# Gating and output taken into the last feed-forward chunk in place, and that chunk's layer norm issued within the chunk ahead of it

## The chip, the cores and the metric

The kernel runs on one core of a Trainium2 chip. The metric is the device time of one execution in microseconds (us), lower is better. A core has five engines that run their own instruction streams and meet at semaphores: TensorE (PE in the rows; its weight loads are PEld), VectorE (DVE), ScalarE (ACT), GpSimd (POOL) and SyncE (SP), which here only issues DMA transfers. Matrix products land in PSUM, everything else lies in SBUF.

## The reference, cut to what matters

Four sequences of 1024 tokens with 256 features go through a layer norm, then two branches: a global attention over all tokens, and a stack of two local layers. The branch outputs meet in a gate.

```python
# x: (4, 1024, 256)
xn = layernorm(x)
s = attn(xn, w_qkv, w_out)           # global attention, 16 heads
t = xn
for l in range(2):                   # the local layers
    t = t + local_attention(shift_token(t)) @ wo[l]
    h = shift_token(t)
    h = (h - mean(h)) / sqrt(var(h) + 1e-05) * lg + lb
    a, g = split(h @ w1 + b1)        # 2 * 682 columns
    t = t + (a * gelu(g)) @ w2 + b2
out = x + s * silu(t)
```

The names are shortened here; the last line is the part that the change moves.

## The kernel before, in words

The 4096 tokens are 8 chunks of 512 columns (`CHUNKS`), each four windows of 128. The stream `t` is held transposed, features on partitions, in `xnt`, a tile of 2 halves (`KD`) by 8 chunks by 513 columns. Four stages follow each other: `prepare_tokens`, `global_attention`, `local_layers` and `combine`. Between two stages stands a barrier of all engines, and the tiles of a stage are given back at its end.

**local_layers.** Its loop runs over rounds g. A round has four window steps w = 0 to 3. Round g projects the queries, keys and values of chunk g (of 16, 8 for each of two layers), works its attention, and does the second half, the feed-forward part, of chunk g - 2. So the last two rounds, g = 16 (`LAST`) and g = 17, project nothing: round 16 still has the ends of the last attention windows and the feed-forward part of the layer's chunk 6, and round 17 has only the feed-forward part of chunk 7. `PLAN` lists the rounds, and in each engine's `body` hand-written conditions say what that engine issues in a step, and in what order. There is no scheduler: the order of the code is the order of the engine.

The feed-forward part of a chunk, by its functions: `output_product` (8 products of `wo` with the attention output into PSUM banks `ffn0`, `ffn1`), `add_attention` (VectorE, sum with `xnt` into `mid`), `mean` (a product with `mean_w`), `centre` (VectorE), `square_deviations` (ScalarE), `variance` (a product), `inverse_deviation` (ScalarE, Ln then Exp with scale -0.5), `scale` and `shift` (VectorE, on `centred`, then a split into `f_high` and `f_low`), five `hidden_tile`s f = 0 to 4, each with 6 products into `ffn0` for the gate half and 6 into `ffn1` for the other, `tails` (6 products), and two `down`s m = 0, 1 with 6 products each. ScalarE turns each gate half by Gelu (`gate_tile`), VectorE multiplies (`hidden_tile`), and `add_ffn` adds the down product to `mid` and writes it to `xnt`. The fp32 products (`wo`, `mean_w`, `w2`) are two instructions each in the rows, those of the split operands one. In round 17 each of these steps waits for the one before it.

**The two PSUM banks** go round: `ffn_ready` and `ffn_taken` count the fills and the reads of each bank, with 9 uses of bank 0 and 8 of bank 1 in a round (`USES`). A fill waits until its bank's last use was taken.

**combine** starts after the barrier. SyncE loads the attention output `s` of chunks 6 and 7 and `x` of chunks 6 and 7 (the other six of each were loaded during the last rounds into the places of weights and tables no longer needed, `early_s` and `early_x`). ScalarE makes silu of each half of a chunk, VectorE multiplies half 0 with `s` and GpSimd half 1 (`gated`), TensorE turns the 8 squares of 128 by 128 back into PSUM, VectorE adds `x` into `result`, and SyncE stores 512 KB of output. `silu`, `gated`, `result` and the PSUM tiles have two buffers each, so chunk n waits for chunk n - 2, in `result` for its store.

## Time and profile before

| | us |
|---|---|
| median of 3 runs | 2339.86 |
| lowest, highest | 2337.14, 2340.36 |
| the profiled execution | 2328.96 |
| its span, first to last instruction | 2327.2 |
| its mean granted TensorE clock | 0.971 of full speed |

| engine | busy us | share of the span |
|---|---|---|
| TensorE | 2195.7 | 94% |
| VectorE | 1621.7 | 70% |
| ScalarE | 1380.5 | 59% |
| GpSimd | 610.5 | 26% |

The span counts from the first instruction to the last; the profiled execution's own time has 1.8 us around it. All the times inside a kernel below are us from the start of the span. A row gives start, duration, engine, line and operation, output and inputs, and in brackets the idle time of the engine before it and what ended that. Instructions of an engine overlap a little: two VectorE operations of 0.69 take 1.29 together. "x8" joins eight instructions of a kind.

### The profile page before, as it was taken

The numbers are of one execution on the slowest core, as the hardware profiler recorded it, in microseconds if no ns is written. First come the engines' busy times: TensorE is split into PE (matmuls) and PEld (weight loads), VectorE is DVE, ScalarE is ACT, GpSimd is POOL, SyncE is SP. The second block draws the span as 40 slices with busy tenths as digits, with TensorE's granted clock in tenths as the row PEclk, the third lists the DMA queues.
The fourth block names the chain that finished last, engine by engine and source line by source line (L and its number), as shares of the span: only waits on it lengthen the run. The fifth ranks groups of instructions, "written<-read, shape, count | busy, mean of one in ns | idle before, by whom it ended". The sixth has DMA issues, their size and how long they took to land. (4 is left out here: it accounts for less than half of the span.)

```text
span 2327.2 us, 43427 instructions
## 1 busy us (share of the span) xinstructions
PE 2195.7 (94%) x14592; PEld 1288.5 (55%) x14592; DVE 1621.7 (70%) x3789; ACT 1380.5 (59%) x2551; POOL 610.5 (26%) x490
## 2 busy tenths in 40 slices
PE   7869999999999979899999999899999999999976
PEld 4533333333333336566666666666666676676644
DVE  5768999999999936655666666556666656666534
ACT  2215888888888845555655555555555565565533
POOL 3521200000000024333332333332432333333201
PEclk9977999999999989999999999999999999999988
DMA  4585122211112022200000000000100000000303
GB/s 135 183 252 159 52 64 65 65 56 60 57 53 63 29 80 103 88 10 1 1 0 0 0 0 0 27 1 10 36 1 1 1 0 0 0 0 0 108 1 109
DMA packets 76984, 108.96 MB, mean 47 GB/s; under 512 B 14204, under 2 KB 49360, under 8 KB 76752
## 3 DMA queue, kind: packets, MB, share of 16 engines
q1 hardware_dynamic: 76864, 107.30, 14.4%
q8 instruction: 82, 1.34, 0.3%
q14 instruction: 38, 0.31, 0.0%
HBM read 68.74 MB, written 43.95 MB: 48 GB/s over the span
## 5 line engine op out<-in xcount | busy, mean ns | idle before, releaser
L669 DVE TENSOR_REDUCE maxima<-ps_m 128x1 f32<-128x512 f32 x1024 | 629.1, 683 | 20.7 <-PE ps_m L549 16.6
L737 ACT ACTIVATE probs<-ps_st 128x1024 f32<-128x1024 f32 x512 | 521.1, 1025 | 161.7 <-PE ps_st L576 142.6
L549 PE MATMUL ps_m<-k_st,q_st 48*128 48x512 f32 x1024 | 392.4, 466 | 19.9 <-DMA k_st<-ks 15.6
L1355 ACT ACTIVATE l_probs<-l_probs,l_neg_max 128x256 f32<-128x256 f32 x512 | 254.0, 498 | 194.5 <-DVE l_neg_max L1514 194.5
L576 PE MATMUL ps_st<-q_st,k_st 50*128 50x512 f32 x1024 | 367.5, 444 | 2.0 <-DMA q_st<-max_rows 1.6
L592 PE MATMUL ps_o<-probs,v_st 128*32 128x256 f32 x4096 | 322.1, 392 | 0.1
L1514 DVE CUSTOM_DVE_ANT_1 l_probs<-ring,l_mask 128x256 f32<-128x256 f32 x384 | 140.0, 421 | 198.5 <-PE ring L1123 198.0
L576 PEld LDWEIGHTS ps_st<-q_st,k_st 50*128 50x128 f32 x1024 | 154.5, 186 | 194.0 <-issue 173.8
L1334 ACT COPY p_turned<-ring 128x512 f32<-128x512 f32 x256 | 140.4, 599 | 163.7 <-PE ring L1083 163.6
L1042 POOL TENSOR_SCALAR clipped<-sumsq 128x16 f32<-128x16 f32 x64 | 16.2, 253 | 766.9 <-DVE sumsq L1481 766.9
L549 PEld LDWEIGHTS ps_m<-k_st,q_st 48*128 48x128 f32 x1024 | 166.7, 190 | 53.3 <-DVE maxima L669 31.5
L1044 POOL TENSOR_TENSOR inv_norm<-clipped,halves 128x16 f32<-128x16 f32 x64 | 187.6, 2931 | 5.3
L592 PEld LDWEIGHTS ps_o<-probs,v_st 128*32 128x32 f32 x4096 | 84.1, 108 | 169.5 <-ACT probs L737 110.4
L1573 DVE SCALAR_TENSOR_TENSOR hidden<-ffn,b_l,gate 128x512 f32<-128x512 f32 x96 | 71.9, 749 | 147.2 <-PE ffn L1137 72.3
L1137 PE MATMUL ffn<-hidden,w_l 128*128 128x512 f32 x384 | 172.6, 600 | 0.0
L1526 DVE TENSOR_SCALAR l_probs<-l_probs,l_inv_total 128x256 f32<-128x256 f32 x512 | 166.3, 388 | 4.5
L1046 POOL TENSOR_TENSOR rope_a<-rope_a,rope_b 128x1024 f32<-128x1024 f32 x64 | 157.0, 2453 | 0.0
L1083 PE MATMUL ring<-l_ident,l_probs 128*128 128x128 f32 x1024 | 142.2, 280 | 13.6 <-DVE l_probs L1526 13.6
L1095 PE MATMUL l_ps_o<-p_turned,v_ring 128*64 128x128 f32 x2048 | 149.5, 284 | 5.3 <-ACT p_turned L1334 5.3
L1137 PE MATMUL ffn<-f_high,w_high 128*128 128x512 f32 x352 | 148.1, 421 | 5.7 <-DVE f_low L1564 5.6
L1095 PEld LDWEIGHTS l_ps_o<-p_turned,v_ring 128*64 128x64 f32 x2048 | 110.2, 138 | 66.0 <-issue 53.3
L508 POOL TENSOR_TENSOR max_hl<-row_max,zeros 128x16 fp32r<-128x16 f32 x32 | 7.1, 222 | 531.8 <-DVE row_max L678 531.8
(156 smaller groups left out, 3864.7 us busy)
## 6 DMA issues: line engine op xcount, KB each, us to landing
qs<-split SPq DMA_DIRECT2D x16, 512.0 KB, 3.5
ks<-split SPq DMA_DIRECT2D x16, 512.0 KB, 5.1
q_st<-qs SPq DMA_DIRECT2D x64, 128.0 KB, 2.5
k_st<-ks SPq DMA_DIRECT2D x64, 128.0 KB, 3.1
o<-o_sb SPq DMA_DIRECT2D x32, 256.0 KB, 2.3
hidden<-o SPq DMA_DIRECT2D x17, 256.0 KB, 6.6
x_in<-in_L_attn_x_dram SPq DMA_DIRECT2D x8, 512.0 KB, 5.6
v<-v_sb SPq DMA_DIRECT2D x16, 256.0 KB, 4.7
```

The costliest lines, as they stand in the source:

```text
L549: nc.tensor.matmul(bank(base, use)[:, :], q_st[u][r, qt * P:(qt + 1) * P], k_st[u][r, h * CH:(h + 1) * CH], start=True, stop=True).then_in ...
L576: mm = nc.tensor.matmul(ps_st[j][:, h * CH:(h + 1) * CH], k_st[u][r, kt * P:(kt + 1) * P], q_st[u][r, h * CH:(h + 1) * CH], start=True, st ...
L592: mm = nc.tensor.matmul(ps_o[r:r + 32, q], v_st[:, kt, 2 * u + j, :], probs[:, kt % 4, j, h * CH + q.start:h * CH + q.stop], start=(kt == ...
L669: nc.vector.tensor_reduce(maxima[:, par, side(e), tile + e // 4, e % 2:e % 2 + 1], bank(base, k + e)[:, :], AX_X, ALU.max).then_inc(m_used, 1)
L737: nc.scalar.activation(probs[:, kt % 4, j, :], ps_st[j][:, :], ACT.Exp, scale=float(G_DIM) ** -0.5).then_inc(exp_done, 1)
L1044: nc.gpsimd.tensor_tensor(inv_norm[:, :], clipped[:, :], halves[:, :], ALU.pow).then_inc(inv_done, 1)
L1046: nc.gpsimd.tensor_tensor(rope_a[:, :, :], rope_a[:, :, :], rope_b[:, :, :], ALU.add).then_inc(added, 1)
L1083: mm = nc.tensor.transpose(ring[(PT + p) % 2][:, (2 * j + s) * P:(2 * j + s + 1) * P], probs[:, 2 * p + j, s * P:(s + 1) * P], wt.ident[:, :])
L1095: mm = nc.tensor.matmul(ps_o[j * HDIM:(j + 1) * HDIM, p * P:(p + 1) * P], v_ring[:, slot, head * HDIM:(head + 1) * HDIM], p_turned[:, p % ...
L1137: mm = nc.tensor.matmul(ffn[bank][:, :], a, b, start=(n == 0), stop=(n == len(operands) - 1))
L1355: nc.scalar.activation(probs[:, head, :], probs[:, head, :], ACT.Exp, bias=neg_max[:, head:head + 1], scale=-1.0, accum_out=total[:, head: ...
L1526: ins = nc.vector.tensor_scalar(probs[:, head, :], probs[:, head, :], inv_total[:, head:head + 1], None, ALU.mult)
```

## The change

Three things are done, all in `local_layers`, and the stage `combine` is gone, with the barrier ahead of it.

- **The layer norm of chunk 7** is issued within round 16. `late(g)` is true for round 17, and then the steps from `output_product` to `shift` use other places: PSUM `ps_q`, `ps_k`, `ps_v` and `l_ps_o` in the place of `ffn0` and `ffn1`, `l_mid` (in the attention's `probs`), `l_centred` (`qk_n`), squares in `k_ring`, and `h_high`, `h_low` for `f_high`, `f_low`. TensorE has `late_output` after hidden tile 3 of round 16, `late_mean` after its tails, and `late_variance` between its two downs.
- **The gate** is written in place: silu and the product with `s` both overwrite `xnt`. ScalarE makes silu of chunks 0 to 3 at the end of round 16, and of chunks 4 to 7 at the end of round 17. GpSimd multiplies both halves of chunks 0 to 3 and half 1 of chunks 4 to 6, VectorE half 0 of chunks 4 to 6 and both of chunk 7. `s` of chunks 6 and 7 goes to `o_ring`, `x` of them to `v_ring`.
- **The turning back, the sum and the store** of chunks 0 to 5 stand between the products of round 17: `turn_back(n)` on TensorE, `add_x(n)` on VectorE, in place into the room of `x`, from where SyncE stores. Two of the four PSUM tiles are the attention's `ring0` and `ring1`, two are `ps_q` and `ps_k`.

Two loads of ScalarE's function table (in round 16 at w = 2, and in round 17) are left out, and three others (silu, Gelu, silu) stand where the silus are.

```diff
+        def nth(g, bank, use):
+            return (g - 2) * USES[bank] + use - (2 if late(g) else 0)
+        back = ((ring[0], ring[1]), (ps_q, ps_k))
...
                 run(pool, body)
+                for n in range(4):
+                    for k in range(KD):
+                        gate_back(n, k)
+                for n in range(4, CHUNKS - 1):
+                    gate_back(n, 1)
...
                         if forward and w == 3:
                             hidden_tile(g, lf, 4)
+                        if late(g) and w == 3:
+                            turn_back(2)
...
                         if forward and w == 2:
                             hidden_tile(g, lf, 2)
+                        if late(g) and w == 2:
+                            turn_back(0)
                         if forward and w == 3:
                             tails(g, lf)
+                        if late(g) and w == 3:
+                            turn_back(3)
...
                         if forward and w == 2:
                             hidden_tile(g, lf, 3)
+                        if last_but_one and w == 2:
+                            late_output()
+                        if late(g) and w == 2:
+                            turn_back(1)
+                        if last_but_one and w == 3:
+                            late_mean()
                         if forward and w == 3:
                             down(g, lf, 0)
+                        if late(g) and w == 3:
+                            turn_back(4)
+                            turn_back(5)
+                        if last_but_one and w == 3:
+                            late_variance()
...
                         if forward and w == 3:
                             down(g, lf, 1)
+                        if late(g) and w == 3:
+                            turn_back(6)
+                            turn_back(7)
...
+                for n in range(CHUNKS):
+                    sp.wait_ge(summed, 2 * n + 2)
+                    dst = out[n // 2, n % 2 * CH:(n % 2 + 1) * CH, :].rearrange("(t p) n -> p t n", p=P)
+                    sp.dma_start(dst, x_room(n)).then_inc(out_stored, 16)
...
-                        if w >= 2 and forward:
+                        if w >= 2 and forward and (mid_ or isinstance(g, int) and g == LAST and w == 3):
                             nc.scalar.preload_act_table_set(EXP_LN)
...
+                        if isinstance(g, int) and g == LAST and w == 3:
+                            square_deviations(g + 1)
+                            inverse_deviation(g + 1)
+                            nc.scalar.preload_act_table_set(SILU)
+                            for n in range(4):
+                                silu(g, n)
+                            nc.scalar.preload_act_table_set(GELU)
+                        if late(g) and w == 3:
+                            nc.scalar.preload_act_table_set(SILU)
+                            for n in range(4, CHUNKS):
+                                silu(g, n)
...
+                def gate_back(n, k):
+                    attention_in(dve, n)
+                    dve.wait_ge(silu_done[k], n + 1)
+                    nc.vector.tensor_tensor(xnt[:, k, n, 1:], attention(n, k), xnt[:, k, n, 1:], ALU.mult).then_inc(gated_done[k], 1)
+
+                def add_x(n):
...
+                    for m in range(2):
+                        dve.wait_ge(turned_back, 2 * n + m + 1)
+                        room = x_room(n)[:, 2 * m:2 * m + 2, :].rearrange("p t n -> p (t n)")
+                        nc.vector.tensor_tensor(room, back[n % 2][m][:, :], room, ALU.add).then_inc(summed, 1)
...
+                        if late(g) and w == 3:
+                            add_x(0)
                         if forward and w == 3:
                             hidden_tile(g, lf, 4)
...
+                        if late(g) and w == 3:
+                            add_x(1)
                         if forward and w == 3:
                             hidden_tile(g, lf, FT)
+                        if late(g) and w == 3:
+                            add_x(2)
+                            add_x(3)
+                            for k in range(4, CHUNKS - 1):
+                                gate_back(k, 0)
...
                         if forward and w == 3:
                             add_ffn(g, lf, n, 0)
+                        if late(g) and w == 3:
+                            add_x(4)
+                            gate_back(CHUNKS - 1, 0)
+                            add_x(5)
+                        if last_but_one and w == 3:
+                            scale(g + 1, lf)
+                            shift(g + 1, lf)
+                        if forward and w == 3:
                             add_ffn(g, lf, n, 1)
-                            carry(g, n)
+                            if late(g):
+                                add_x(6)
+                                gate_back(CHUNKS - 1, 1)
+                                add_x(7)
+                            else:
+                                carry(g, n)
```

TensorE at the end of chunk 6 and the start of chunk 7, before. `ffn<-o_ring,wo_l` is the output product, the two with `mean_w` are mean and variance, `ffn<-hidden,w_l` are the downs, and `ffn<-f_high,w_high` with `normed` opens chunk 7's hidden tile 0.

```order
L1137 MATMUL ffn<-hidden,w_l 128x512 [waits ffn_taken0,ffn_taken1]
...
L1137 MATMUL ffn<-o_ring,wo_l 128x512 [waits ffn_taken0,o_out]
...
L1137 MATMUL ffn<-mid,mean_w 128x512 [waits ffn_taken0,ffn_taken1]
...
L1137 MATMUL ffn<-hidden,mean_w 128x512 [waits ffn_taken1,sq_dev]
...
L1137 MATMUL ffn<-f_high,w_high 128x512 [waits ffn_taken0,normed]
```

The same place in the changed kernel:

```order
L1221 MATMUL ps_q<-o_ring,wo_l 128x512 [waits l_roped,o_out]
...
L1221 MATMUL ps_v<-l_probs,mean_w 128x512 [waits late_mid,v_out]
...
L1199 MATMUL ffn<-hidden,w_l 128x512 [waits ffn_taken1]
...
L1221 MATMUL l_ps_o<-k_ring,mean_w 128x512 [waits sq_dev]
...
L1199 MATMUL ffn<-hidden,w_l 128x512 [waits ffn_taken0,ffn_taken1]
...
L1199 MATMUL ffn<-h_high,w_high 128x512 [waits ffn_taken0,normed]
```

The three products of the norm now stand ahead of the second down, and nothing stands between that down and chunk 7's first tile but the wait for `normed` and bank 0.

VectorE at the same place in the changed kernel, from the centring of chunk 7 on. The last `xnt<-ffn` row is `add_ffn(16, 1)`, which frees bank 0.

```order
L1728 SCALAR_TENSOR_TENSOR qk_n<-ps_v,l_probs 128x512 [waits late_ready]
...
L1763 SCALAR_TENSOR_TENSOR xnt<-ffn,b_l,mid 128x512 [waits ffn_ready1]
L1737 TENSOR_TENSOR qk_n<-qk_n,dev 128x512 [waits sq_dev,dev_done]
...
L1742 TENSOR_SCALAR qk_n<-qk_n,lnp_l 128x512 [waits l_scaled] x2
L1746 CAST h_high<-qk_n 128x512 [waits shifted_done] x2
L1749 TENSOR_TENSOR h_low<-qk_n,h_high 128x512 [waits f_high_done] x2
L1763 SCALAR_TENSOR_TENSOR xnt<-ffn,b_l,mid 128x512 [waits ffn_ready0]
```

The scaling, shifting and splitting of chunk 7 stand between chunk 6's two sums, and chunk 6's second sum stands behind them.

ScalarE in the changed kernel, at the turn from round 16 to 17, from the Ln of chunk 7's variance (`dev<-l_ps_o`) and the Exp behind it to the first Gelu of chunk 7.

```order
L1512 ACTIVATE dev<-l_ps_o,eps_col 128x512 [waits late_ready]
L1518 ACTIVATE dev<-dev 128x512 [waits late_ln]
L1592 ACT_TABLE_LOAD
L1526 ACTIVATE xnt<-xnt 128x512 [waits x_out] x8
L1595 ACT_TABLE_LOAD
L1533 ACTIVATE gate<-ffn,b_l 128x512 [waits ffn_ready0] x5
```

Eight silus and two table loads now stand ahead of the first Gelu. GpSimd's first eight products wait for one of these silus each, and for nothing else that is late.

## Rows read from the trace of the kernel before

**Rows 1.** Busy time in four stretches: stretch, length, engines, TensorE clock, DMA.
```profile
2223.10:2249.20 26.10, 26.10 (x92) 16.77 (x90) 5.26 (x7) 9.85 (x11) 0.00 (x0) 1.00 0.00 0
2249.20:2270.70 21.50, 11.66 (x25) 4.31 (x24) 7.86 (x15) 3.75 (x5) 0.00 (x0) 0.84 0.00 1
2270.70:2298.40 27.70, 27.65 (x90) 17.98 (x90) 5.26 (x7) 7.98 (x9) 0.00 (x0) 0.94 0.00 0
2298.40:2327.20 28.80, 11.77 (x64) 9.55 (x64) 18.07 (x26) 10.31 (x17) 11.19 (x8) 0.73 0.66 219
```

**Rows 2.** Chain that ended last, by line, of 2200 to 2327.
```profile
by line: DMA out_dram<-result 9.8%; DVE result L1756 2.3%; PE ps_t L1776 1.5%; issue 1.1%; ACT L1725 1.0%; POOL gated L1734 1.0%; ACT silu L1725 0.9%; DVEq L1703 0.5%; DVEq L1755 0.1%; DVE gated L1743 0.0%; POOLq L1731 0.0%
```

**Rows 3.** Timeline: TensorE's products of rounds 16 and 17.
```profile
2203.30 1.88 PE L1137 MATMUL ffn<-mid,mean_w 128*128 128x512 f32 x4
...
2223.11 0.50 PE L1137 MATMUL ffn<-f_high,w_high 128*128 128x512 f32 x1
...
2234.44 0.50 PE L1137 MATMUL ffn<-f_high,w_high 128*128 128x512 f32 x1
...
2238.76 10.46 PE L1137 MATMUL ffn<-hidden,w_l 128*128 128x512 f32 x24
...
2250.15 7.10 PE L1137 MATMUL ffn<-o_ring,wo_l 128*128 128x512 f32 x16 [0.94 <-DVE xnt L1578]
```

**Rows 4.** Timeline: chunk 7's norm, from the variance product on.
```profile
2262.60 2.58 PE L1137 MATMUL ffn<-hidden,mean_w 128*128 128x512 f32 x4 [2.56 <-ACT hidden L1368]
...
2265.23 0.69 ACT L1374 ACTIVATE dev<-ffn,eps_col 128x512 f32<-128x512 f32 x1 [2.67 <-PE ffn L1137]
2265.95 0.63 ACT L1376 ACTIVATE dev<-dev 128x512 f32<-128x512 f32 x1
...
2266.61 1.29 DVE L1552 TENSOR_TENSOR hidden<-hidden,dev 128x512 f32<-128x512 f32 x2 [5.24 <-ACT dev L1376]
...
2268.73 0.75 DVE L1561 CAST f_high<-hidden 128x512 fp32r<-128x512 f32 x2
2269.40 1.28 DVE L1564 TENSOR_TENSOR f_low<-hidden,f_high 128x512 fp32r<-128x512 f32 x2
...
2270.74 0.79 PE L1137 MATMUL ffn<-f_high,w_high 128*128 128x512 f32 x1 [5.55 <-DVE f_low L1564]
```

**Rows 5.** Timeline: VectorE and GpSimd at once, in combine, then in prepare_tokens.
```profile
2302.40 1.27 POOL L1734 TENSOR_TENSOR gated<-wqkv_high,silu 128x512 f32<-128x512 f32 x1 [117.37 <-ACT silu L1725]
2302.88 1.34 DVE L1743 TENSOR_TENSOR gated<-wqkv_high,silu 128x512 f32<-128x512 f32 x1 [0.35 <-ACT silu L1725]
2303.63 1.73 POOL L1734 TENSOR_TENSOR gated<-wqkv_high,silu 128x512 f32<-128x512 f32 x1
...
63.82 0.40 DVE L195 TENSOR_SCALAR xn<-x_in,moments,rstd 128x256 f32<-128x256 f32 x1
...
63.94 0.76 POOL L150 COPY xnt<-xs 128x512 f32 x1
64.14 0.70 DVE L195 TENSOR_SCALAR xn<-x_in,moments,rstd 128x256 f32<-128x256 f32 x1
...
64.64 0.68 POOL L150 COPY xnt<-xs 128x512 f32 x1
...
64.76 0.70 DVE L195 TENSOR_SCALAR xn<-x_in,moments,rstd 128x256 f32<-128x256 f32 x1
```

**Rows 6.** Timeline: ScalarE's table load and silus at the start of combine.
```profile
2299.81 1.28 ACT L1725 ACT_TABLE_LOAD   x1 [9.70 <-PEq L1022]
...
2301.11 3.78 ACT L1725 ACTIVATE silu<-xnt 128x512 f32<-128x512 f32 x7
```

**Rows 7.** TensorE alone, columns as in Rows 1: its clock and instructions.
```profile
2270.00:2272.00 2.00, 1.26 (x3) 0.50 0.00 0
2272.00:2274.00 2.00, 2.00 (x6) 0.50 0.00 0
2274.00:2276.00 2.00, 2.00 (x10) 0.98 0.00 0
```

**Rows 8.** Timeline: chunk 7's last sum, a chunk's transposes, the last output sums.
```profile
2298.43 0.75 DVE L1578 SCALAR_TENSOR_TENSOR xnt<-ffn,b_l,mid 128x512 f32<-128x512 f32 x1 [4.40 <-PE ffn L1137]
...
2309.60 1.09 PE L1776 MATMUL ps_t<-l_ident,gated 128*128 128x128 f32 x8 [0.53 <-DVE gated L1743]
...
2320.90 2.56 DVE L1756 TENSOR_TENSOR result<-ps_t,x_late 128x512 f32<-128x512 f32 x4 [2.60 <-issue]
```

More of the change, by code:

```diff
@@ L1186, in body @@
                 def body(g, la, lf, before_hidden=None):
+                    last_but_one = isinstance(g, int) and g == LAST
                     for w in range(WPC):
@@ L1202, in body @@
                             turn_probs(W, 1)
-                        if forward and w == 0:
+                        if forward and w == 0 and not late(g):
                             output_product(g, lf)
@@ L1215, in body @@
                             turn_probs(W, 3)
-                        if forward and w == 0:
+                        if forward and w == 0 and not late(g):
                             mean(g)
@@ L1242, in body @@
                             project_o(W - 1)
-                        if forward and w == 0:
+                        if forward and w == 0 and not late(g):
                             variance(g)
@@ L1420, in body @@
                             take_o(g, w)
-                        if forward and w == 0:
+                        if forward and w == 0 and not late(g):
                             square_deviations(g)
@@ L1598, in body @@
                             before_hidden()
-                        if forward and w == 1:
+                        if forward and w == 1 and not late(g):
                             scale(g, lf)
@@ L1613, in body @@
                             take_next(g, la, lf)
-                        if forward and w == 0:
+                        if forward and w == 0 and not late(g):
                             add_attention(g, n)
```

268 lines of the change are left out of this document (143 added, 125 removed).

## The prediction, made before the changed kernel ran

> **What bounds the kernel now.** The change touches only the last 104 us, so I read from the end backwards. The chain of work that ended last shows what the last stage waits for: output stores, 9.8% of the last 127 us, with short pieces of sum, transpose and gate between them [rows 2]. So `combine` is bound by its own pipeline of two buffers, not by one engine. Then the busy times by stretch [rows 1]: chunk 6's tiles and downs take 26.1 us with TensorE full, 21.5 us follow in which TensorE is busy 11.66 (product, sum, mean, centring, variance and norm of chunk 7, one after the other), then 27.7 us of chunk 7's tiles and downs, again full, and 28.8 us from the last down product to the end, in which no engine is busy more than 18.07. The change fills the second stretch and the fourth. The four give 104.1 us, and I work out each anew.
>
> **First stretch: it takes in the norm's products.** Hidden tiles 0 to 3 run from 2223.11 to 2234.44 and the 24 instructions of the downs take 10.46, so 0.43 each [rows 3]. An instruction with `wo` or `mean_w` costs the same: 16 in 7.10, 4 in 1.88 with its overlap. Output product, mean and variance are 16 + 4 + 4 = 24 instructions, 10.3 us, all on TensorE's path. Do they wait? The output product needs only the attention, done before 2223. The mean product needs two VectorE sums, done about 1 us behind the output product, while hidden tile 4 and the tails fill 4.3 us (2234.44 to 2238.76, [rows 3]). The variance needs centring (1.4) and squares (1.2), and the first down, 5.2 us, covers them. So no wait: 26.1 + 10.3 = 36.4 us, and the second down ends at 2249.2 + 10.3 = 2259.5. If a cover were too short by 1 us, it would cost 1 us.
>
> **Second stretch: the gap before chunk 7.** Behind the variance product come Ln, Exp and eight VectorE instructions: from 2265.23 to 2269.40 + 1.28 = 2270.68, 5.45 us [rows 4]. Behind them VectorE has `add_ffn(16, 1)`, 0.75, which frees bank 0, so 6.2 us. The second down covers 5.2 of this. Undisturbed, TensorE would stand 1.1 us.
>
> But it is not undisturbed. Behind Exp ScalarE loads the silu table (1.28) and makes its first silu (0.63), and GpSimd starts 0.14 later [rows 6, 5]: 2.1 us behind Exp, just as the two casts and the two subtractions of the split are due (they begin 2.15 us behind Exp's end, [rows 4]). Two rows show what follows. A VectorE product of two SBUF tiles, begun at 2302.88 while GpSimd's ran from 2302.40 to 2303.67, took 1.34 and not 0.68, and GpSimd's next took 1.73 and not 1.27: they ran one behind the other. In `prepare_tokens` two GpSimd copies and VectorE's TENSOR_SCALARs alternate: VectorE's pitch becomes 0.62 where 0.32 is normal (63.82 to 64.14) [rows 5]. So when both have instructions queued, they take turns. GpSimd has eight products in a row, since silus come every 0.54 (7 in 3.78, [rows 6]) and a product takes 1.27. Four VectorE instructions each behind one of them: 4 x 1.2 = 4.8 us. The bounds: 0, if none is held, and 8 x 1.27 - 2 = about 8 us, if GpSimd lets none through. I take 4.8, since both rows show turns. `add_ffn` and `add_x` have PSUM on one side and are not held: the sums among GpSimd's products took the usual time (2.56 for four, [rows 8]).
>
> The gap is 1.1 + 4.8 = 5.9 us and chunk 7's tiles start at 2265.4 instead of 2270.7. After the old gap of 5.55 us TensorE stood at the lower of its two levels, 1.2 GHz (clock 0.50), till 2274, with 0.43 for an instruction instead of 0.23 for the first eight: 1.6 us, contained in the 27.7 [rows 7]. A gap of 5.9 brings the same again, so nothing changes there.
>
> For the table load the row shows the silu 1.30 us behind its start [rows 6]. The Trainium skill, "ScalarE: Activation LUTs", section "What ACT_TABLE_LOAD costs", adds a drain of about 1.38 us to it, about 2.66 us in all. Where a load has that drain, GpSimd starts behind the split and the sum is 2316.6; that is the fourth case below.
>
> **Third stretch: chunk 7 with six transposes inside.** `turn_back(0)` to `(5)` stand ahead of the second down's end; one takes 1.05 (8 instructions in 1.09 with their overlap, [rows 8]): 6.3 us, all on TensorE's path. 27.7 + 6.3 = 34.0. Their inputs: GpSimd has gated chunks 0 to 3 by about 2270, the first `turn_back` comes near 2275. For chunks 4 to 6 silu begins behind the last Gelu, about 2288, and VectorE must, in its order, finish `add_x(2)`, `add_x(3)` (1.29 each), three gates (0.55 to 1.8 each), `add_ffn(17, 0)`, `add_x(4)`, the gate of chunk 7's half 0 and `add_x(5)` before `add_ffn(17, 1)`, due at 2299.4. Adding these up gives 2298.5: 0.9 us to spare. Queued behind the new waits for `turned_back` in front of hidden tiles 4 and tail are just these products, for which TensorE's first down waits; the transposes come 1 to 3 us earlier, so I cost it at nothing, and at up to 5.7 us if the list runs late. The silus, Gelu loads and GpSimd's eleven products lie beside TensorE's work. SyncE's queue has stores behind loads that were issued long before.
>
> **Fourth stretch: what stays behind the last product.** `add_ffn(17, 1)` 0.75; `add_x(6)` 1.29, which hides the last silu (0.63); the gate of half 1, 0.68; four transposes and their handover 0.65; `add_x(7)` 1.29; from the last sum to the end 3.74 as before (2320.90 + 2.56 = 2323.46, the end at 2327.2, [rows 8]). That is 8.4, less some overlap 8.2, against 28.8. Gone with it are the barrier, the loads of chunks 6 and 7 (issued in round 16, among idle queues) and the wait of `result` for its stores: stores now have a place each.
>
> **The sum.** 36.4 + 5.9 + 34.0 + 8.2 = 84.5 against 104.1: 19.6 us less. The span goes to 2307.6, the profiled execution from 2328.96 to about 2309.4. The median of the runs lies 10.9 us above the profiled execution; I carry that over: 2339.86 - 19.6 = 2320.3.
>
> **The rivals.**
> 1. *They take turns in the split* (forecast): 2320.3, with 2317 to 2323 for its own terms. For it, both rows of [rows 5].
> 2. *The split is not held*, because VectorE's four instructions pass in one turn or GpSimd begins a little later. The gap is about 1 us, and the clock need not fall: 4.8 + 1.6 less, 2313.9. For it: GpSimd's start is only 0.1 us ahead of the casts. Against: the silus follow each other at 0.54 and GpSimd is behind with them throughout.
> 3. *VectorE's list in chunk 7 becomes the bound*: three gates held by GpSimd's again, in front of sums for which TensorE waits. Up to 5.7 us more, 2326. For it: 0.9 us to spare in a list of 11 us. Against: at the tiles of chunk 7 VectorE is busy 5.26 of 27.7 [rows 1].
> 4. *The table load's drain*, a mechanism by which ScalarE is free again only some 1.4 us behind the row's end of a load. Worked out from rows: GpSimd begins that much later, behind the last instruction of the split, so 4.8 + 1.6 are saved; but the first Gelu comes 2 x 1.4 us later, about 2.7 us late for bank 0. 2313.9 + 2.7 = 2316.6. The row's 0.02 us between load and silu speaks against it. The Trainium skill's section named above would have it so.
> 5. *Slower: the lower clock stays for chunk 7.* If short transposes and stalls keep TensorE at 1.2 GHz from 2265 to the end, 66 tile products take 0.2 more each, 24 of the downs 0.43 and 56 transposes 0.13: 31 us, of which 1.6 is already in. 2349. It decides the sign when the low level lasts for two thirds of the chunk. Against: after the same gap the level came back in 3.3 us [rows 7].
> 6. *It does not do what it says*: tiles of chunk 7 wait as late as before and the output still comes in a row behind them; within 0.2% of before. Against: the order of the instructions.
>
> **How the numbers follow.** Chances: 1: 0.52; 2: 0.22; 3: 0.15; 4: 0.03; 5: 0.03; 6: 0.05. What a measurement of this kernel can tell from no change is about 0.2%, 4.7 us. Cases 1 to 4 are faster by more than that, 0.92; case 6 is the same, 0.05; case 5 slower, 0.03. The range leaves out cases 5 and 6 and reaches from case 2 less 3 us to case 3 plus 3 us: 2311 to 2329, some 0.9 of the chance by the cases, cut to 8 in 10 by what moves between executions (3.2 us in three runs).
>
> **What would show it.** Right: a TensorE gap of 5 to 7 us before chunk 7's first tile, ended by VectorE; the two casts or two subtractions there taking 2 to 4 us instead of 2.0 together; 34 us from there to the last down; about 8 us from there to the end. A gap near 1 us is case 2; VectorE's gates ending a wait of a down or of `turn_back(4)` to `(6)` is case 3; a clock of 0.50 beyond 2270 is case 5. It is wrong altogether if stages before 2223 change in length, since no instruction of them does.

## The result, and the profile after

The changed kernel took 2307.01 us (median of four runs, 2300.86 to 2311.05), the kernel before, beside it, 2338.5 (2330.63 to 2340.36). The ratio of the runs is put at 0.9878, with a 95% interval of 0.9854 to 0.9901: 28.5 us less (the two medians lie 31.5 apart), where the prediction had 19.6 less. The direction was right, the size too small, and the time lies below the range of 2311 to 2329.

The profiled execution of the changed kernel took 2310.06 us, with a span of 2308.3. These are its four stretches, cut as in [rows 1] (columns as there): hidden tiles and downs of chunk 6 with the norm's products, gap, tiles and downs of chunk 7, the rest.

```profile
2231.70:2267.90 36.20, 36.20 (x116) 21.40 (x114) 11.80 (x20) 13.39 (x19) 1.58 (x1) 1.00 0.09 29
2267.90:2269.15 1.25, 0.09 (x1) 0.03 (x1) 1.14 (x3) 1.25 (x3) 1.25 (x1) 1.00 0.00 0
2269.15:2300.40 31.25, 31.25 (x140) 22.03 (x141) 17.35 (x24) 11.22 (x17) 12.57 (x11) 1.00 0.26 88
2300.40:2308.30 7.90, 1.96 (x16) 1.48 (x14) 3.90 (x6) 0.63 (x1) 0.00 (x0) 0.88 0.56 189
```

Together 76.6 us against 104.1: 27.5 less, nearly what the runs show. The prediction had 36.4, 5.9, 34.0 and 8.2, or 84.5. So the missing 7.9 us are 4.65 in the gap, 2.75 in chunk 7, 0.3 at the end and 0.2 at the start.

Yet the two spans differ by 18.9 only (2327.2 and 2308.3). The first tile of chunk 6 starts at 2231.67 in this trace and at 2223.11 in [rows 3], and nothing ahead of it is touched by the change. The difference lies between 200 and 300 us. The first line is from the trace of before, the second from that of after:

```profile
200.00:300.00 100.00, 99.57 (x949) 39.67 (x945) 97.42 (x169) 82.96 (x84) 23.34 (x26) 1.00 0.27 81
200.00:300.00 100.00, 99.74 (x853) 38.37 (x849) 87.92 (x151) 74.03 (x75) 23.31 (x26) 0.88 0.21 65
```

TensorE is full in both, but the granted clock is 0.88 and not 1.00, and 96 fewer of its instructions got done. Cut finer, both traces have a clock of 0.50 (1.2 GHz) from 190 to 195 us and of 1.00 (2.4 GHz) from 230 on. What differs is when it rises: between 195 and 200 us before, between 220 and 225 after.

The forecast's doubtful place is the gap ahead of chunk 7. The timeline of the changed kernel's trace shows it (start, duration, engine, line, operation, tiles; in brackets the idle time ahead and who ended it). The two lines in the middle with x2 are the casts and the subtractions of the split:

```profile
2264.25 1.28 ACT L1592 ACT_TABLE_LOAD   x1
2265.47 0.54 DVE L1742 TENSOR_SCALAR qk_n<-qk_n,lnp_l 128x512 f32<-128x512 f32 x1
2265.54 0.63 ACT L1526 ACTIVATE xnt<-xnt 128x512 f32<-128x512 f32 x1
2265.93 0.54 DVE L1742 TENSOR_SCALAR qk_n<-qk_n,lnp_l 128x512 f32<-128x512 f32 x1
2266.32 2.97 POOL L1112 TENSOR_TENSOR xnt<-wqkv_high,xnt 128x512 f32<-128x512 f32 x1 [72.56 <-ACT xnt L1526]
2266.39 0.76 DVE L1746 CAST h_high<-qk_n 128x512 fp32r<-128x512 f32 x2
2267.06 1.29 DVE L1749 TENSOR_TENSOR h_low<-qk_n,h_high 128x512 fp32r<-128x512 f32 x2
2268.26 0.74 DVE L1763 SCALAR_TENSOR_TENSOR xnt<-ffn,b_l,mid 128x512 f32<-128x512 f32 x1
2269.15 0.47 PE L1199 MATMUL ffn<-h_high,w_high 128*128 128x512 f32 x1 [1.16 <-DVE xnt L1763]
2269.26 1.10 POOL L1112 TENSOR_TENSOR xnt<-wqkv_high,xnt 128x512 f32<-128x512 f32 x1
```

GpSimd came where the prediction had it, 0.07 us ahead of the first cast. But VectorE's four instructions took 2.0 us in all, as without it, and GpSimd's product lasted 2.97 instead of 1.1: it ended 0.94 behind the last subtraction. TensorE stood 1.16 us. That is the second case of the prediction (2313.9), to which it gave 0.22.

Some 25 us later, in round 17, the same two engines did take turns, that is, each instruction of one waited for one of the other. VectorE's gate `L1710`, unhindered 0.68, came while GpSimd's product was on. The last line is `add_ffn(17, 1)`, the sum that must not come late:

```profile
2291.34 1.02 DVE L1710 TENSOR_TENSOR xnt<-wqkv_low,xnt 128x512 f32<-128x512 f32 x1
2291.77 1.54 POOL L1112 TENSOR_TENSOR xnt<-wqkv_low,xnt 128x512 f32<-128x512 f32 x1
2292.28 1.57 DVE L1710 TENSOR_TENSOR xnt<-wqkv_low,xnt 128x512 f32<-128x512 f32 x1
2293.27 1.72 POOL L1112 TENSOR_TENSOR xnt<-o_ring,xnt 128x512 f32<-128x512 f32 x1
2293.78 1.76 DVE L1710 TENSOR_TENSOR xnt<-o_ring,xnt 128x512 f32<-128x512 f32 x1
...
2300.43 0.75 DVE L1763 SCALAR_TENSOR_TENSOR xnt<-ffn,b_l,l_probs 128x512 f32<-128x512 f32 x1 [1.24 <-PE ffn L1199]
```

So two questions go to the chip: is the gain in the changed part alone, and what decides between turns and none?

### The profile page after: what moved, and what is told of

The parts are those of the page before. It is cut to its first block, busy times and chain, and to the rows that moved or that the text cites. A ratio compares the mean times of both kernels' runs of the same rounds, so it can differ in the third digit from the quotient of the medians.

```text
span 2308.3 us, 43409 instructions
## 1 busy us (share of the span) xinstructions
PE 2197.8 (95%) x14592; PEld 1287.6 (56%) x14592; DVE 1620.2 (70%) x3785; ACT 1375.1 (60%) x2547; POOL 614.2 (27%) x493
## 3 DMA queue, kind: packets, MB, share of 16 engines
q8 instruction: 82, 1.34, 0.2%
## 4 chain that ended last, share of the span: by engine, by line
PE 51%; DVE 2%; issue 1%; ACT 1%; DVEq 0%; ACTq 0%
PE ffn L1199 24%; PE l_ps_o L1157 5%; PE ring L1145 5%; PE ring L1185 4%; PE ps_v L1132 3%; PE ps_q L1132 3%; PE ps_k L1132 2%; PE ring L1169 2%; PE ring L1187 1%; DVE l_probs L1675 1%; PE ring L1188 0%; ACT k_ring L1481 0%; DVE l_probs L1687 0%; ACT l_probs L1489 0%; PE ps_k L1221 0%
## 5 line engine op out<-in xcount | busy, mean ns | idle before, releaser
L549 PE MATMUL ps_m<-k_st,q_st 48*128 48x512 f32 x1024 | 398.2, 472 | 19.8 <-DMA k_st<-ks 15.6
L576 PE MATMUL ps_st<-q_st,k_st 50*128 50x512 f32 x1024 | 373.3, 450 | 2.3 <-DMA q_st<-max_rows 1.9
L592 PE MATMUL ps_o<-probs,v_st 128*32 128x256 f32 x4096 | 327.4, 398 | 0.1
L1104 POOL TENSOR_TENSOR qk_n<-rope_a,inv_norm 128x1024 f32<-128x1024 f32 x64 | 123.1, 1924 | 84.4 <-PE ring L1169 74.1
```

Of the source, the lines that this page charges most:

```text
L549: nc.tensor.matmul(bank(base, use)[:, :], q_st[u][r, qt * P:(qt + 1) * P], k_st[u][r, h * CH:(h + 1) * CH], start=True, stop=True).then_in ...
L576: mm = nc.tensor.matmul(ps_st[j][:, h * CH:(h + 1) * CH], k_st[u][r, kt * P:(kt + 1) * P], q_st[u][r, h * CH:(h + 1) * CH], start=True, st ...
L592: mm = nc.tensor.matmul(ps_o[r:r + 32, q], v_st[:, kt, 2 * u + j, :], probs[:, kt % 4, j, h * CH + q.start:h * CH + q.stop], start=(kt == ...
```

## Experiments on where the gain is

**The changed kernel again.**

> The changed kernel once more, beside the others, as their control. If the 27.5 us between the two traces (from chunk 6's first tile to the end, 104.1 before and 76.6 after) are what the change gives, that stretch is 76 to 77.5 us again, whatever the stages before it take in this execution, and the time is 26 to 30 us under the kernel before's. If instead the 8.6 us by which the stages before chunk 6's tiles were longer in the changed kernel's trace are a cost of the change, chunk 6's first tile starts near 2231.7 again and not near 2223.

It took 2303.74 us against 2332.84, ratio 0.9877 (0.9848 to 0.9907). Its first tile of chunk 6 starts at 2225.38, its span is 2302.0: 76.6 us again, with 36.31, 1.16, 31.25 and 7.90. Between 200 and 300 us its clock was 0.98.

In the eight traces of this study that hold the whole computation, the start of chunk 6's tiles goes with this one number: clock 1.00, start 2223.1; 0.98, 2225.0 and 2225.4; 0.95, 2226.7; 0.91, 2229.7; 0.87 to 0.89, 2231.7 to 2233.0. All runs' spans agree: those of the kernel before, less 104.1, put this start at 2221 to 2233, and those of the changed kernel, less 76.6, at 2222 to 2233 (an estimate that takes the last stretches as fixed). The 8.6 us are thus an execution's own, and no cost of the change. What decides when this clock rises in an execution, no run here shows.

**The norm ahead, the output stage as before.** Everything of the gating is taken out of the last chunk, and `combine` put back:

```diff
-                for n in range(4):
-                    for k in range(KD):
-                        gate_back(n, k)
...
-                        if late(g) and w == 3:
-                            add_x(0)
...
+            combine(nc, wt, x, x_early, xnt, s_dram, s_stored, out)
```

> The layer norm of chunk 7 ahead, in its new places, and the output stage as it was before (silu, product, transposes and sums in a stage of their own behind the last chunk). By the additive theory the four stretches are 36.2, 1.3, 26.1 (27.7 less the 1.6 of the lower clock, and no transposes) and 28.8: 92.4 against 104.1, so 11.7 us less than before. A rival: with no silu table load and no products of GpSimd beside VectorE's norm chain the gap is shorter than 1.25 us (below 1.0), if these had cost anything there.

The cut shows only a part: all silus, products with `s`, transposes, sums and stores are out of `local_layers`. It took 2320.55 us, ratio 0.9943 (0.9925 to 0.9962). The stretches:

```profile
2232.35:2268.67 36.32, 36.32 (x116) 21.45 (x114) 11.89 (x20) 11.02 (x14) 0.00 (x0) 1.00 0.00 0
2268.67:2269.82 1.15, 0.00 (x1) 0.03 (x1) 1.04 (x3) 0.00 (x0) 0.00 (x0) 1.00 0.00 0
2269.82:2295.76 25.94, 25.94 (x90) 16.84 (x90) 5.45 (x8) 4.12 (x6) 0.00 (x0) 1.00 0.00 1
2295.76:2323.00 27.24, 12.39 (x65) 10.49 (x64) 18.77 (x26) 10.30 (x17) 11.34 (x8) 0.77 0.69 231
```

They add up to 90.65 us, 13.4 less than before (11.7 were expected). The gap is 1.15 without a product of GpSimd and without a silu: they cost nothing there. Chunk 7 takes 25.94, and 27.7 less the 1.6 of the lower clock is 26.1. With this row the changed kernel's 31.25 gives the price of the six groups of transposes: 5.31, 0.89 each. The output stage took 27.24 and not 28.8. The chains that ended last differ there by one output store: in the kernel before it lasts 4.36 us (from 2317.73), while no store of norm_only's chain lasts over 2.91. Why that one was long stays open.

**Gating in place, the norm where it was.**

```diff
+                        if late(g) and w == 0:
+                            late_output()
+                            late_mean()
+                            late_variance()
...
-                        if last_but_one and w == 2:
-                            late_output()
...
+                            nc.scalar.preload_act_table_set(EXP_LN)
+                            square_deviations(g + 1)
+                            inverse_deviation(g + 1)
```

> Silu, product, transposes and sums within chunk 7, its layer norm where it was before (behind the silus of chunks 0 to 3). By the additive theory: 26.1, 21.5, 27.7 + 6 x 0.87 = 32.9 and 7.9: 88.4 against 104.1, 15.7 us less; with norm_only's 11.7 this is the whole 27.5. Against that: GpSimd's eight products now run beside the norm's VectorE instructions from its first sums on, not beside the last ones. If whoever streams first holds the other in turns, the norm's VectorE instructions of two SBUF tiles (centring's and split's) take 1.3 to 1.8 instead of 0.7, and the second stretch is 24 to 27 us.

It took 2315.76 us, ratio 0.9918 (0.9892 to 0.9944). The first stretch is 26.02, the last 7.83, and the two between them:

```profile
2259.05:2278.85 19.80, 10.81 (x25) 4.05 (x23) 8.49 (x15) 3.75 (x5) 1.64 (x2) 0.96 0.01 1
2278.85:2312.47 33.62, 33.62 (x140) 23.88 (x141) 17.17 (x23) 9.27 (x14) 4.28 (x3) 0.92 0.24 81
```

That is 87.3 us in all, 16.8 less (15.7 were expected). The silus ran at 2250.79 and GpSimd's products were over at 2260.7, ahead of the norm's instructions (from 2262.5 on), so nothing was held, and the dearer second stretch that its expectation allowed for did not come. This run tells nothing of turns. Its first product of GpSimd, after 56.61 us of idleness, took 1.09: the 2.97 in the changed kernel is no slow start. The second stretch is 1.7 shorter than before. Of this 0.94 is the wait ahead of the output product [rows 3], which is gone since the norm's products have banks of their own. Another 0.6 is the variance product: 1.98 us at a clock of 1.00, against 2.58 before [rows 4], where the clock fell to 0.62 in its course. The gap ahead of chunk 7 is 5.55, as before, and chunk 7 pays the lower clock again: 33.62.

The two halves give 13.4 and 16.8, the whole 27.5. The 2.7 too many are the 1.6 of norm_only's output stage and the 1.7 of gate_only's second stretch, less 0.6 in chunk 7. The gain is where the prediction put it.

## Experiments on who waits for whom

**VectorE and GpSimd alone.** VectorE's streams of eight against GpSimd's five products.

> Nothing of the computation is left but a copy of x to the output; beside it VectorE and GpSimd run streams against each other: eight VectorE instructions on 128x512 float32 tiles of one kind (products back to back; products each waiting for its predecessor; copies to fp32r; two copies and two subtractions in turn; TENSOR_SCALARs; products with one operand in PSUM) against five GpSimd products of SBUF tiles, once with VectorE ahead by two instructions and once with GpSimd ahead by one. Theory A (the kind decides: VectorE's back-to-back instructions let none of GpSimd's through): VectorE's mean is 0.65 to 0.70 in the phases with both orders and GpSimd's first product lasts as long as VectorE's stream. Theory B (who streams first decides): with VectorE ahead its instructions take their usual time and GpSimd's wait; with GpSimd ahead VectorE's take 1.3 to 1.8. Theory C (turns always, as forecast): both orders show VectorE at 1.3 to 1.8 and GpSimd at 1.7. With an operand in PSUM all expect VectorE undisturbed.

They took turns in every phase but those with an operand in PSUM, whoever came first. These rows are from the products that each wait for the one before and from the casts, GpSimd coming second in both:

```profile
24.62 0.69 DVE L59 TENSOR_TENSOR v_plain<-va,vb 128x512 f32<-128x512 f32 x1
25.34 0.69 DVE L59 TENSOR_TENSOR v_plain<-va,vb 128x512 f32<-128x512 f32 x1
25.48 1.67 POOL L88 TENSOR_TENSOR g_res<-ga,gb 128x512 f32<-128x512 f32 x1 [4.58 <-DVE v_plain L59]
26.07 1.63 DVE L59 TENSOR_TENSOR v_plain<-va,vb 128x512 f32<-128x512 f32 x1
...
46.10 0.42 DVE L65 CAST v_rounded<-va 128x512 fp32r<-128x512 f32 x1
46.36 1.28 POOL L88 TENSOR_TENSOR g_res<-ga,gb 128x512 f32<-128x512 f32 x1 [4.42 <-DVE v_rounded L65]
46.44 1.48 DVE L65 CAST v_rounded<-va 128x512 fp32r<-128x512 f32 x1
```

With one operand in PSUM VectorE's eight took 4.87 us, 0.61 each as against 0.60 before GpSimd came, and ten products of GpSimd 12.46, that is 1.25 each: neither was held. This is theory C, the forecast's picture, and not what the changed kernel shows at the split. Something else had to differ there.

**The norm's own list.**

> Nothing of the computation is left but a copy of x to the output; beside it, ten times over, VectorE runs the last nine instructions of the norm with the kernel's shapes and its own waits (two products, two TENSOR_SCALARs, two casts, two subtractions, one sum with PSUM: 0, 0.6, 1.2, 1.7, 2.1, 2.5, 2.8, 3.4, 4.0 us from the start, 4.7 in all), and GpSimd three products, begun when a ScalarE copy of growing width ends (0.4 to 3.3 us from the start), with four ScalarE copies of 128x512 beside them. Theory 1 (turns whenever both have something queued, as in the first streams): every VectorE instruction of two SBUF tiles that comes behind a GpSimd product lasts 1.0 to 1.8, GpSimd's first product never over 1.9, and the chain takes 4.7 + 3 x 1.1 = 8 us. Theory 2 (an instruction of GpSimd that comes while VectorE's short ones, casts of 0.33 and TENSOR_SCALARs of 0.46 pitch, are on stays behind all of them): when it begins between 1.2 and 2.8 us, GpSimd's first product lasts until the last subtraction is over (up to 3 us) and VectorE's take their usual time; when it begins earlier, during the products, they take turns.

Both patterns came out. GpSimd coming at VectorE's third instruction (start 25.85) is let in; coming at the fourth (33.92) it stays behind all four that follow:

```profile
25.73 0.54 DVE L59 TENSOR_SCALAR qk_n<-qk_n,lnp 128x512 f32<-128x512 f32 x1
25.85 1.36 POOL L86 TENSOR_TENSOR xnt<-early,xnt 128x512 f32<-128x512 f32 x1 [3.98 <-ACT delay L74]
26.18 1.32 DVE L59 TENSOR_SCALAR qk_n<-qk_n,lnp 128x512 f32<-128x512 f32 x1
...
33.83 0.54 DVE L59 TENSOR_SCALAR qk_n<-qk_n,lnp 128x512 f32<-128x512 f32 x1
33.92 3.27 POOL L86 TENSOR_TENSOR xnt<-early,xnt 128x512 f32<-128x512 f32 x1 [4.07 <-ACT delay L74]
34.28 0.42 DVE L62 CAST h_high<-qk_n 128x512 fp32r<-128x512 f32 x1
...
35.56 0.68 DVE L65 TENSOR_TENSOR h_low<-qk_n,h_high 128x512 fp32r<-128x512 f32 x1
```

In the changed kernel GpSimd came at the fourth (2266.32, the second TENSOR_SCALAR began at 2265.93). Theory 2 holds by its numbers, but not by its reason: the run ports had shown that casts alone don't keep GpSimd out. Is it the kind of instruction, what follows, or how many came before? The next runs release GpSimd behind the first, the second, and so on of VectorE's instructions, so release 5 means that it comes while the sixth is on.

> Again only a copy of x to the output, and beside it streams of nine VectorE instructions on 128x512 tiles, each stream eight times: GpSimd's first of two products is released when the first, second, ... eighth of them is done. The kinds: products; casts; casts and subtractions; the norm's list (two products, two TENSOR_SCALARs, two casts, two subtractions, a sum with PSUM) without its own waits, with them, with six ScalarE copies beside it, and with GpSimd's tile shifted by one element. In the stream of norm instructions of the run before, GpSimd was let in when it came in the first three instructions, and stayed behind all the rest when it came in the fourth or later. Theory N (the length of VectorE's unbroken stream decides): in every kind the first product of GpSimd lasts at most 1.9 when released by instruction 1 or 2, and until the end of the stream when released by 4 to 8 (in the stream of products, released by 4, 1.1 + 4 x 0.6 = 3.5 us). Theory K (the kinds of instruction behind it decide: it is the casts of 0.33 pitch, or the PSUM sum at the end): the products' stream lets it in at every release, the norm's list does not from release 3 on. Theory W (the self-waits, ScalarE's work or the shifted tile decide): the norm's list without them lets it in at every release.

GpSimd's first product, by the number of VectorE instructions done when it was released (1 to 8): in the stream of products 1.57, then 1.55 up to the fifth, 2.76, 2.16, 1.55; in casts 1.28 up to the fifth, 1.96, 1.62, 1.28; in casts and subtractions up to 1.55, from the sixth 2.49, 1.89, 1.29. In the norm's list 1.55, 1.41, and from the third 3.28, 2.83, 2.49, 2.15, 1.56, 1.26, with its own waits, ScalarE's copies or the shifted tile all the same within 0.02. Theory W falls. N is nearest, with a limit it did not foresee, and the list reaches it earlier.

> As the run before (only a copy of x to the output, and streams of VectorE instructions with two GpSimd products released behind the k-th): there GpSimd's first product was let in at once, unless few instructions of VectorE were left: two in streams of nine products or nine casts, four ahead of a PSUM sum in the norm's list. Streams now: 12 products; 6 products; 8 products and a PSUM sum; 8 casts and a PSUM sum; the norm's list without the sum; the norm's list with the sum and four products behind it; 4 products, a PSUM sum, 4 products. Theory E (what is left of the stream decides, with the end, a wait for GpSimd, near): in 12 products it is let in at releases 1 to 8 and blocked from 9 on; in 6 products let in at 1 and 2, blocked from 3 on. Theory N (the length already run decides): 12 products are blocked from release 6 on, 6 products never. Theory F (a VectorE instruction without a port within five behind the running one blocks it): 8 products and a sum are let in at releases 1 to 2 and blocked from 3 on, the list with four more products is blocked at releases 3 to 7 and let in again behind the sum; the list without the sum behaves like the streams of products. Let in means 1.25 to 1.7 us for the first product, blocked 2.0 to 3.5.

In 12 products it was let in up to release 5 and blocked from 6 on, until the last product (4.56 us, then 0.6 less for each later release). In 6 products it was never blocked. So it is the length already run (theory N); what is left (E) and a PSUM sum ahead (F) don't matter. The rows of releases 5 and 6 in 12 products, and of release 3 in the list without a sum:

```profile
43.88 1.55 POOL L82 TENSOR_TENSOR first<-ga,gb 128x512 f32<-128x512 f32 x1 [6.86 <-DVE tt_plain L62]
53.96 4.56 POOL L82 TENSOR_TENSOR first<-ga,gb 128x512 f32<-128x512 f32 x1 [6.86 <-DVE tt_plain L62]
...
257.44 3.28 POOL L82 TENSOR_TENSOR first<-ga,gb 128x512 f32<-128x512 f32 x1 [3.78 <-DVE chain_plain L64]
```

A PSUM sum in the middle (release 5 behind it: 3.35) does not start the count anew, and seems to count for two.

> As the two runs before (a copy of x, and streams of nine VectorE instructions with two GpSimd products released behind the k-th). There GpSimd was let in up to release 5, while the sixth instruction was on, and blocked from the seventh on, whatever followed; only where TENSOR_SCALARs with two per-partition operands, or a sum with one, stood in the stream was it blocked earlier. Theory C: such instructions count more than one (three with two per-partition operands, two with one, by those runs), and the limit is a count of six. Then: nine TENSOR_SCALARs with two numbers are blocked from release 6 on; nine with two per-partition operands from release 2 on; nine with one from release 3 on; one with two ahead of eight products, and as the third among products, from release 4 on; one with one ahead of eight products from release 5 on. Rival D: a change of the kind of instruction, not its operands, brings the block forward: then all uniform streams are blocked from release 6 on and both mixed ones earlier. Let in means 1.25 to 1.7 us for GpSimd's first product, blocked 1.9 to 5, up to the end of the stream.

The mixed streams came out as theory C has it, to the instruction. One TENSOR_SCALAR with two per-partition operands, first or third among products: let in up to release 3, blocked from 4 on (3.96). With one such operand: from 5 on (3.36). With two numbers, nine of them: from 6 on (1.96). But nine with two per-partition operands let GpSimd in at every release (1.40, only the seventh 1.86), and nine with one likewise (1.34, 1.74). There theory C fails, and rival D would have it blocked from the sixth on and fails too. So: a count of six, in which a per-partition operand adds one, holds for all streams of these three runs except the uniform ones of that kind. Why those are different stays open. The rows are of releases 3 and 4 with one TENSOR_SCALAR ahead of eight products, and of release 6 among nine TENSOR_SCALARs, each with two per-partition operands:

```profile
159.13 1.55 POOL L85 TENSOR_TENSOR first<-ga,gb 128x512 f32<-128x512 f32 x1 [4.91 <-DVE tt_plain L61]
167.27 3.96 POOL L85 TENSOR_TENSOR first<-ga,gb 128x512 f32<-128x512 f32 x1 [4.91 <-DVE tt_plain L61]
...
79.34 1.40 POOL L85 TENSOR_TENSOR first<-ga,gb 128x512 f32<-128x512 f32 x1 [3.77 <-DVE chain_plain L63]
```

The count also fits the split: at release 3 the norm's list stands, with the instruction that is on, at two products and two TENSOR_SCALARs of three each, that is eight. That the changed kernel's split is this case rests on the copied list, in which GpSimd comes at the same place and is held nearly as long (3.27, and 2.97 in the kernel); no run moves it by one instruction in the kernel itself.

**The turns brought about in the kernel.** The silus of chunks 0 to 2 go ahead of the norm's Ln, so that GpSimd is already streaming when VectorE begins:

```diff
+                            nc.scalar.preload_act_table_set(SILU)
                             square_deviations(g + 1)
+                            for n in range(3):
+                                silu(g, n)
+                            nc.scalar.preload_act_table_set(EXP_LN)
                             inverse_deviation(g + 1)
                             nc.scalar.preload_act_table_set(SILU)
-                            for n in range(4):
-                                silu(g, n)
+                            silu(g, 3)
```

> The silus of chunks 0 to 2 ahead of the norm's Ln and Exp (one more load of each table, 2 x 1.28 us on ScalarE, there idle), the silus of chunk 3 behind them: GpSimd is then in the middle of its first six products when VectorE's norm chain begins. By the rule that both take turns whenever both have something queued, the products, casts and subtractions of the chain are held, up to 1.1 us each, as long as GpSimd has products left: six products from about 9 us ahead of the chain end about 1 us ahead of it or into it, so 0 to 3 of the eight are held, 0 to 3 us in the gap ahead of chunk 7, 1.2 to 4.5. By the rival, that VectorE passes whatever GpSimd does in this place, the gap stays 1.2 and the four stretches 36.3, 1.2, 31.2 and 7.9.

```profile
2257.86 1.72 POOL L1112 TENSOR_TENSOR xnt<-wqkv_high,xnt 128x512 f32<-128x512 f32 x1
2258.37 1.76 DVE L1740 TENSOR_TENSOR qk_n<-qk_n,dev 128x512 f32<-128x512 f32 x1
2259.62 1.63 POOL L1112 TENSOR_TENSOR xnt<-wqkv_low,xnt 128x512 f32<-128x512 f32 x1
2260.05 1.48 DVE L1745 TENSOR_SCALAR qk_n<-qk_n,lnp_l 128x512 f32<-128x512 f32 x1
...
2265.61 0.65 PE L1199 MATMUL ffn<-h_high,w_high 128*128 128x512 f32 x1 [4.35 <-DVE xnt L1766]
2266.06 0.63 PE L1199 MATMUL ffn<-h_low,w_high 128*128 128x512 f32 x1
```

The second product and both TENSOR_SCALARs (the other one 1.48 too) are held a full turn, the first product by 0.2. The gap is 4.35, and behind it the lower clock holds for eight matmuls (0.43 apart and not 0.23), so that chunk 7's stretch is 32.79. The four stretches give 81.3, 4.7 more than the changed kernel. This is the forecast's mechanism in a kernel where GpSimd comes early: a turn cost 0.94 to 1.1 us, where the forecast had 1.2, and three instructions were held, where it had four.

**GpSimd held back.** `pool.wait_ge(normed, KD * LAST)` ahead of its first product.

> GpSimd's first product waits for the last subtraction of the norm of chunk 7; nothing else is changed. If GpSimd's first product lasted 2.97 us because VectorE held it, it now lasts 1.1 to 1.3, begins some 2 us later (when the last subtraction is done) and ends within 0.4 us of where it ended. If the 2.97 were GpSimd's own (72 us of idleness ahead of it), it stays near 2.9 and ends 2 us later. The four stretches stay 36.3, 1.2, 31.2 and 7.9 in both.

```profile
2263.42 1.09 POOL L1112 TENSOR_TENSOR xnt<-wqkv_high,xnt 128x512 f32<-128x512 f32 x1 [74.81 <-DVE h_low L1750]
```

The product took 1.09 after 74.81 us of idleness, so 1.9 of the 2.97 were waiting. The stretches are 36.33, 1.16, 31.23 and 7.82: no difference that matters.

**The end in halves.** In the last list on VectorE the gate goes between the two sums of chunk 6, and the last two chunks are stored by halves:

```diff
-                                add_x(6)
+                                add_x(6, (0,))
                                 gate_back(CHUNKS - 1, 1)
+                                add_x(6, (1,))
                                 add_x(7)
```

> The end of the list on VectorE put in another order (first sum of chunk 6, gate of chunk 7's half 1, second sum of chunk 6, sums of chunk 7), and the outputs of chunks 6 and 7 stored in halves, each behind its own sum. In the changed kernel the last stretch is 7.9: sum of the layer 0.75, two sums 1.29, gate 0.68, transposes, sums 1.29, last store. The gate comes 0.6 earlier, and the last transposes with it; the last store carries half as much: the last stretch is 6.5 to 7.4 us instead of 7.9. A rival: half a store takes as long as a whole one (its fixed part decides) and two more stores queue on the same engine, so the stretch stays within 0.3 us of 7.3 (the gate's part alone), or 7.9.

```profile
2298.42:2305.40 6.98, 1.96 (x16) 1.49 (x14) 4.00 (x6) 0.63 (x1) 0.00 (x0) 0.84 0.64 214
```

The last stretch is 6.98 instead of 7.90, and the other three are unchanged (36.31, 1.16, 31.25): 0.9 us less by the trace. About 0.4 is the gate's (the wait of the last transposes is 1.00 and not 1.39), 0.5 the store's (2.85 from the last sum's end to the end of the span, 3.37 before). The runs, 2303.14 us with ratio 0.9876 (0.9857 to 0.9895), can't tell it from the changed kernel. It is the best version by its stretches, not shown so by its times.

## Why the prediction was right and wrong

- **First stretch, 36.4:** measured 36.20. All covers held, no product waited.
- **Second stretch, 5.9:** measured 1.25. This step failed: "they take turns" for the four instructions of the split, 4 x 1.2 = 4.8 us in the sum. They were not held at all (2.0 us together); GpSimd's product waited behind them instead. The undisturbed 1.1 and the start of GpSimd 0.07 us ahead of the casts were right. But both places of [rows 5] show VectorE at the start of a stream: a lone gate at 2302.88, and copies in turn with single TENSOR_SCALARs. The split stands in fifth to eighth place of one, and there GpSimd is kept out. I had taken turns for a property of the two engines; in the streams measured it depends on how far VectorE's has got. The price of a turn was about right (1.0 us in pool_first, 1.2 in the sum), and so was what follows it, a gap long enough for the clock to fall.
- **Third stretch, 34.0:** measured 31.25. The forecast holds 1.6 for the lower clock, which followed from the gap and fell with it: the clock was 1.00 throughout ([rows 7] has the old drop). Another 1.0 is the transposes, a term that was mis-sized: 0.89 and not 1.05 a group, 5.3 and not 6.3. I had used a group's length alone, where the next matmul in fact begins 0.79 to 0.88 behind its start.
- **Third case, VectorE's list as the bound:** the gates of round 17 were held (1.02, 1.57 and 1.76 instead of 0.68), and it did not matter: the last sum still waited 1.24 us for TensorE. So there were some 1.2 us to spare with the holds in, where I had 0.9; rival 3 falls.
- **Sums with PSUM, "not held":** right, but not by the row given. The four sums of [rows 8] at 2320.90 run after GpSimd's last product, which ended at 2317.63. What shows it is ports (0.61 each beside GpSimd) and round 17, where the sum begun at 2290.74 took its usual 0.68 beside GpSimd's product of 2290.72.
- **Fourth stretch, 8.2:** measured 7.90.
- **The table load's drain:** the load at 2264.25 took 1.28, and the silu followed at 2265.54, 1.29 behind its start, the first Gelu 1.30 behind the other load. The Trainium skill, "ScalarE: Activation LUTs", section "What ACT_TABLE_LOAD costs", has a drain beside the load; these rows show none. Rival 4 falls.
- **Rivals 5 and 6** fall by the same four stretches: clock 1.00 in chunk 7, transposes within it.
- **From trace to time:** I carried 10.9 us, the median less the profiled execution, over to the changed kernel. Its profiled execution lies 3 us above its median. The 10.9 belonged to one execution of the kernel before, the only trace here with a clock of 1.00 between 200 and 300 us. For the difference of two kernels it did no harm, since I took 19.6 off the median; but a time of one execution of this kernel is known to some 10 us only. With the right stretches the same sum gives 2339.86 - 27.5 = 2312.4, in the range. Of the 5.4 left to 2307.01, 1.4 is the kernel before, whose median beside it was 2338.5, and the rest is within what the runs move (10.2 us from the lowest to the highest of the changed kernel's four).
- The range had its low end at case 2 less 3 us. Case 2 was priced at 6.4 less than the forecast and came at 7.9 with the transposes.

## What to carry to other kernels

Cut the changed part out of both traces at the same instruction and compare lengths there: 76.6 came out again to 0.1 us in two executions whose spans differed by 6. A resource that two engines share is read from a row whose place in the stream is like the one in question, not only its kind: behind a long unbroken stream VectorE kept GpSimd out, at the start of one they alternated. And put the helper's work so that it comes late in the critical engine's stream, or behind it; here GpSimd running already when that stream began, and not joining it 2 us later, cost 4.7 us.

## What the hardware showed beyond what I had expected

- GpSimd's product of 1.1 to 1.3 us is let in between two VectorE instructions of SBUF tiles if it comes no later than during the sixth of an unbroken stream, and waits for the end of the stream from the seventh on (1.55 against 4.56 in twelve products). Per-partition operands bring this forward, by one instruction each, in mixed streams; in uniform ones of that kind they do not.
- When they alternate, a cast that takes 0.42 takes 1.48, and a product of 0.69 takes 1.63 to 1.75. An operand in PSUM frees VectorE's instruction of it (0.61 each beside GpSimd).
- The mean clock between 200 and 300 us was 0.87 to 1.00 in eight traces, by when it rose from 0.50 to 1.00 in them. The start of chunk 6 moved with it by up to 10 us.
